# First front of a two-FFN, one-mixer layer: three groups routed before the shared expert starts, statistics of all tokens early, VectorE takes half of the inverse roots

## Chip, core and metric

The kernel runs on one core of a Trainium2 chip. The metric is the device time of one execution in microseconds (us), lower is better. Engines are called by the names of the profile: PE is TensorE, DVE is VectorE, ACT is ScalarE, POOL is GpSimd, SP is SyncE.

## What is computed

4096 tokens of 128 channels (16 sequences of 256) pass three residual steps, each on a layer norm of the tokens: half an FFN, a causal decaying mixer with two circular transforms, and half of the same FFN again.

```python
def ffn(x):                        # x: (4096, 128), already layer-normed
    logits = x @ router.T          # 8 experts
    idx = argmax(logits)           # one expert for each token
    h = silu(x @ gate[idx].T) * (x @ up[idx].T)          # 256 wide
    y = h @ down[idx].T
    ys = (silu(x @ w_gate_s.T) * (x @ w_up_s.T)) @ w_down_s.T   # shared expert, all tokens
    return y + ys

x = x + 0.5 * ffn(layernorm(x))
x = x + attn(layernorm(x))         # n + gate * corr(decay_scan(conv(n, bind)), unbind)
x = x + 0.5 * ffn(layernorm(x))
```

## The kernel before

Tokens are held in SBUF as 32 tiles of 128, and worked on in 8 groups of 4 tiles (`TPG = 4`, `G = 8`). Every engine has its program written out by hand, with semaphores between them. Each FFN has a **front** and an **expert part**. Here the front of the first FFN matters; it is the function `front(0, k)` of PE, ACT and DVE and `first_ffn(k)` of POOL, called for k from -3 (DVE), -1 (PE, ACT) and so on up to 7. For one group it does this:

- DVE `stats_of` or `moments` and `aggregate`: mean and variance of the four tiles (L591 to L602). In `choose` the four L591 of a later group stand between the linked steps of the routing, so that these hide each other's latency; `AHEAD = 3` says that group k+3 is measured while group k is routed.
- POOL `rstd`: `(variance + eps) ** -0.5` by one power instruction (L367) and the shift (L371).
- ACT `norm`: four normalised tiles `xn` (L463). PE `turn`: four transposes (L871). ACT `evac_rows`: the copy `xnT` (L478).
- PE: four products with the router (L905), semaphore `logits`. DVE `choose` (L662 to L668): the first best expert of each token as a one-hot matrix. PE: ranks of the tokens within their expert (L924 to L932). DVE `place_rows` (L677, L681): the row to which each token goes.
- POOL `scatter`: four indirect DMAs (L378) that put the group's rows into `dispatched`, sorted by expert.

The rank of the next group builds on the counts of this one, and the routing of group k+1 may start only after `place_rows` of group k, which frees the bank `rt`.

The **shared expert** is cut into 24 parts: for every group two halves of gate and up (`part` 0 and 1: PE L885 with two 512-column products, ACT silu L487, DVE product L639) and one down product (`part` 2: PE L893, DVE L607). They stand in the order `SHARED_PARTS`; `parts_at(k, i)` gives those before (`i = 0`) and behind (`i = 1`) the routing of group k. Before, groups 1 to 7 each take one part in either place, 14 in all (`EARLY`); the next five (up to `LATE = 19`) stand behind the front, and the others behind the expert part. The five and DVE's table chain (`block_experts`, `tables`, L750 to L778), which needs the counts of all tokens, are the last thing ahead of the expert part. There PE first waits for these five parts, since the banks are used again (first product L959); SP loads blocks of sorted rows when all scatters have landed.

ACT waits for POOL in `norm`, and every engine takes its instructions in the order written. SP issues the loads of x in four pieces (`X_LOADS`: group 0, group 1, groups 2 and 3, groups 4 to 7), between them the weights.

## Time and profile before

| | |
|---|---|
| median of 3 runs | 345.94 us (343.34 to 346.11) |
| the profiled execution's own time | 345.24 us |
| its span, first to last instruction | 343.5 us |
| mean granted TensorE clock | 0.931 |
| busy: PE, DVE, ACT, POOL | 273.2, 189.6, 160.2, 191.2 us |
| first scatter starts, last one of the first front ends | 13.67, 67.47 us |
| first product of the first expert part starts | 75.05 us |

The busy times are sums over the whole span. The change touches the first 75 us, so the times of the single instructions there tell more than the sums. A name after `<-` in square brackets is what ended an engine's idle time, as far as the profile can tell; `remote` stands where it found no instruction that did.

### The profile page before, as it was taken

The numbers are of one execution on the slowest core, as the hardware profiler recorded it, in microseconds if no ns is written. First come the engines' busy times: TensorE is split into PE (matmuls) and PEld (weight loads), VectorE is DVE, ScalarE is ACT, GpSimd is POOL, SyncE is SP. The second block draws the span as 40 slices with busy tenths as digits, with TensorE's granted clock in tenths as the row PEclk, the third lists the DMA queues.
The fourth block names the chain that finished last, engine by engine and source line by source line (L and its number), as shares of the span: only waits on it lengthen the run. The fifth ranks groups of instructions, "written<-read, shape, count | busy, mean of one in ns | idle before, by whom it ended". The sixth has DMA issues, their size and how long they took to land.

```text
span 343.5 us, 7913 instructions
## 1 busy us (share of the span) xinstructions
PE 273.2 (80%) x1804; PEld 217.7 (63%) x1804; DVE 189.6 (55%) x725; ACT 160.2 (47%) x375; POOL 191.2 (56%) x302
## 2 busy tenths in 40 slices
PE   7788991889799788895499889959797877969860
PEld 2465770559798678763386667735697766859540
DVE  5666640944444354436999898728353524534353
ACT  3534540146555455513599488501564635535210
POOL 6466775404576655662447888764057465655700
PEclk9899998599989999998859989998999999989996
DMA  7931111222222222119000100113222222222178
GB/s 194 379 146 43 40 50 47 88 56 64 63 65 74 65 62 78 56 47 240 5 3 25 41 32 32 49 47 96 58 63 73 65 60 62 70 62 64 41 226 268
DMA packets 34990, 28.34 MB, mean 83 GB/s; under 512 B 4784, under 2 KB 31792, under 8 KB 34704
## 3 DMA queue, kind: packets, MB, share of 16 engines
q1 hardware_dynamic: 25328, 16.06, 16.8%
q0 software_dynamic: 4544, 9.45, 7.6%
q10 hardware_dynamic: 5088, 2.50, 2.4%
q8 instruction: 11, 0.18, 0.2%
q14 instruction: 19, 0.16, 0.2%
HBM read 15.37 MB, written 12.62 MB: 81 GB/s over the span
## 4 chain that ended last, share of the span: by engine, by line
PE 25%; issue 19%; SPq 15%; POOL 11%; DVE 10%; another core or an unknown queue 7%; DMA 7%; ACT 3%; DVEq 1%; POOLq 0%; ACTq 0%
PE bank L959 9%; SPq L304 6%; POOL dispatched L378 6%; PE bank L885 5%; SPq L316 5%; PE bank L893 3%; DMA back<-returned 3%; PE bank L969 2%; PE bank L905 2%; DMA xs<-dispatched 2%; POOL returned L412 2%; POOL scale_f L367 2%; DVE st_f L591 2%; SPq L336 1%
## 5 line engine op out<-in xcount | busy, mean ns | idle before, releaser
L412 POOL DMA_INDIRECT returned<-ey,token x78 | 77.7, 996 | 66.5 <-DVE ey L807 34.0
L959 PE MATMUL bank<-xsT,wgu 128*128 128x128 f32 x624 | 87.3, 285 | 14.9 <-ACT xsT L531 6.0
L959 PEld LDWEIGHTS bank<-xsT,wgu 128*128 128x128 f32 x624 | 77.7, 196 | 19.6 <-issue 9.0
L378 POOL DMA_INDIRECT dispatched<-xn,slot x64 | 64.0, 1000 | 28.2 <-issue 17.7
L885 PE MATMUL bank<-xnT,gu 128*128 128x512 f32 x128 | 67.6, 659 | 2.9 <-issue 1.6
L801 DVE TENSOR_TENSOR eh<-eg,bank 128x256 f32<-128x256 f32 x78 | 32.8, 420 | 57.0 <-ACT eg L538 39.0
L538 ACT ACTIVATE eg<-bank 128x256 f32<-128x256 f32 x78 | 29.8, 382 | 58.1 <-PE bank L959 43.3
L969 PE MATMUL bank<-wdn,eh 128*128 128x128 f32 x312 | 48.7, 281 | 0.8 <-issue 0.7
L487 ACT ACTIVATE sg<-bank 128x512 f32<-128x512 f32 x32 | 18.9, 589 | 64.1 <-PE bank L885 29.2
L512 ACT ACTIVATE wgu<-gu 128x512 f32 x78 | 48.3, 624 | 0.6 <-issue 0.6
L969 PEld LDWEIGHTS bank<-wdn,eh 128*128 128x128 f32 x312 | 41.9, 196 | 1.8 <-issue 1.6
L893 PEld LDWEIGHTS bank<-dn,hs 128*128 128x128 f32 x256 | 33.0, 207 | 11.9 <-DVE hs L639 9.1
L893 PE MATMUL bank<-dn,hs 128*128 128x128 f32 x256 | 34.4, 291 | 6.2 <-DVE hs L639 5.7
L885 PEld LDWEIGHTS bank<-xnT,gu 128*128 128x128 f32 x128 | 23.9, 205 | 23.0 <-issue 22.0
L463 ACT ACTIVATE xn<-xres,shift_f,scale_f 128x128 f32<-128x128 f32 x64 | 26.3, 482 | 18.8 <-POOL shift_f L371 18.8
L785 DVE COPY wdn<-dn 128x256 f32 x78 | 23.5, 302 | 20.6 <-PE bank L969 19.3
L639 DVE TENSOR_TENSOR hs<-sg,bank 128x512 f32<-128x512 f32 x32 | 21.8, 682 | 11.7 <-ACT sg L487 11.6
L807 DVE COPY ey<-bank 128x128 f32<-128x128 f32 x78 | 22.2, 284 | 8.9 <-issue 4.9
L948 PE MATMUL bank<-ident,xs 128*128 128x128 f32 x80 | 18.1, 286 | 10.2 <-DMA xs<-dispatched 9.4
L405 POOL TENSOR_TENSOR token<-xs,to_replica 128x1 int32<-128x1 int32 x78 | 16.3, 209 | 13.0 <-issue 6.1
L905 PEld LDWEIGHTS bank<-routerT,xnT 128*128 128x128 f32 x128 | 17.0, 201 | 9.1 <-issue 7.4
L531 ACT ACTIVATE xsT<-bank 128x256 f32<-128x256 f32 x40 | 14.9, 372 | 12.6 <-PE bank L948 5.8
(102 smaller groups left out, 294.0 us busy)
## 6 DMA issues: line engine op xcount, KB each, us to landing
xs<-dispatched SPq DMA_DIRECT2D x80, 66.0 KB
back<-returned SPq DMA_DIRECT2D x16, 256.0 KB, 5.5
gu<-in_gu SPq DMA_DIRECT2D x1, 2048.0 KB
out<-xres ACTq DMA_DIRECT2D x8, 256.0 KB, 3.9
returned<-ey,token POOLq DMA_INDIRECT x78
dn<-in_dn SPq DMA_DIRECT2D x1, 1024.0 KB
dispatched<-xn,slot POOLq DMA_INDIRECT x64
dispatched<-pads SPq DMA_DIRECT2D x10, 66.0 KB
```

The source lines that it names most:

```text
L378: nc.gpsimd.indirect_dma_start(dispatched[:, :], bass.IndirectOffsetOnAxis(slot[:, i:i + 1], 0), xn[:, i, :], None, bounds_check=last_row) ...
L412: nc.gpsimd.indirect_dma_start(returned[:, :], bass.IndirectOffsetOnAxis(token[:, s:s + 1], 0), ey[:, s, :], None, bounds_check=last_back) ...
L463: nc.scalar.activation(dst[:, at * TPG + t, 0:C], xres[:, i, :], ACT.Identity, bias=shift[kind][:, i:i + 1], scale=scale[kind][:, i:i + 1] ...
L512: nc.scalar.activation(wgu[:, r, :], tile(gu, e), ACT.Copy).then_inc(blk_wgu, 1)
L538: nc.scalar.activation(eg[:, r, :], bank[4 + r][:, 0:H], ACT.Silu).then_inc(blk_silu, 1)
L785: nc.vector.tensor_copy(wdn[:, r, :], tile(dn[:].rearrange("p e h c -> p e (h c)"), e)).then_inc(blk_wdn, 1)
L801: nc.vector.tensor_tensor(eh[:, r, :], eg[:, r, :], bank[4 + r][:, H:2 * H], ALU.mult).then_inc(blk_mul, 1)
L885: last = nc.tensor.matmul(ps[:], gu[:, SHARED, at:at + P], xnT[:, g, :], start=True, stop=True)
L893: last = nc.tensor.matmul(o_ps[:, t * C:(t + 1) * C], hs[:, n % 2, h, t * P:(t + 1) * P], dn[:, SHARED, h, :], start=(h == 0), stop=(h == ...
L905: last = nc.tensor.matmul(rt[:, t * E:(t + 1) * E], xnT[:, k, t * P:(t + 1) * P], routerT[:], start=True, stop=True)
L959: last = nc.tensor.matmul(bank[4 + s % WR][:, i * P:(i + 1) * P], wgu[:, s % WR, i * P:(i + 1) * P], xsT[:, s // 2 % 2, s % 2, :], start=T ...
L969: last = nc.tensor.matmul(bank[2 + s % 2][:, 0:C], eh[:, s % WR, h * P:(h + 1) * P], wdn[:, s % WR, h * C:(h + 1) * C], start=(h == 0), st ...
```

## The change

It touches the first front alone, apart from counts of semaphores:

- `FILL` replaces one part on either side of each routing: in the first front groups 0, 1 and 2 take no shared part, groups 3, 4 and 5 two each, groups 6 and 7 three each (two before the routing, one behind). 12 parts stand in the front and seven behind it. In the second front the parts stay where they were.
- `STATS_AT`: the statistics of groups 0, 1, 2 are taken ahead of the loop as before, group 3 in the routing of group 0, groups 4 and 5 with group 1, groups 6 and 7 with group 2; the second one of each pair stands behind `place_rows`, all four instructions of L604 in a row.
- The inverse roots of groups 0 to 3 are POOL's, all before its first scatter. Those of groups 4 to 7 are computed by DVE in one chain of 12 linked steps over 16 columns (`rstd_of_rest`): a bit trick for the first guess, three Newton steps, the shift. ACT's `norm` of groups 4 to 7 waits for the whole chain. POOL has no root between its scatters any more.
- `prepare_attention` of DVE (with ACT's tanh and the product of the two keys on PE), and PE's wait for the shared weights, move from group 0 to group 3.
- SP issues all x loads, and then the weights of the shared expert.

```diff
-PER_STEP = 2
-EARLY = PER_STEP * (G - 1)
-LATE = EARLY + 5
+FILL = ((0, 0, 0, 2, 2, 2, 3, 3), (0, 2, 2, 2, 2, 2, 2, 2))
+EARLY = tuple(sum(fill) for fill in FILL)
+LATE = max(EARLY) + 5
+STATS_AT = {-3: (0,), -2: (1,), -1: (2,), 0: (3,), 1: (4, 5), 2: (6, 7)}
+SHARED_FROM = 3
+NEWTON = 3
+MAGIC = float(0x5F3759DF)
+BY_DVE = 4
+DVE_RSTD_STEPS = 3 + 3 * NEWTON
...
-            return SHARED_PARTS[PER_STEP * (k - 1) + i:][:1] if 1 <= k < G else []
+            if not valid(k):
+                return []
+            first, middle = sum(FILL[f][:k]), (FILL[f][k] + 1) // 2
+            return SHARED_PARTS[first + i * middle:first + (FILL[f][k] if i else middle)]
...
             load_x(0)
             load_x(1)
             sp.dma_start(routerT[:], router_in).then_inc(routes_in, 16)
+            load_x(2)
+            load_x(3)
             sp.dma_start(gu[:, SHARED, :], gu_in[:, SHARED, :]).then_inc(shared_in, 16)
             sp.dma_start(dn[:, SHARED, :, :], dn_in[:, SHARED, :, :]).then_inc(shared_in, 16)
-            load_x(2)
...
-            load_x(3)
...
             def first_ffn(k):
                 if k < 0:
-                    rstd("f", k + AHEAD, k + AHEAD)
-                elif k in (1, 3):
-                    rstd("f", k + 2, k + 2, groups=2)
-                elif k == 4:
-                    rstd("f", k + 3, k + 3)
-                if valid(k):
+                    rstd("f", k + BY_DVE, k + BY_DVE)
+                else:
                     scatter(0, k)
...
+                if kind == "f" and BY_DVE <= n < G:
+                    act.wait_ge(dve_rstd, DVE_RSTD_STEPS)
...
+            def rstd_of_rest():
+                at = slice(BY_DVE * TPG, NT)
+                v, y, step = var["f"][:, at], scale["f"][:, at], [0]
+                def link(ins):
+                    step[0] += 1
+                    ins.then_inc(dve_rstd, 1)
+                    if step[0] < DVE_RSTD_STEPS:
+                        dve.wait_ge(dve_rstd, step[0])
+                dve.wait_ge(stats["f"], G)
+                link(nc.vector.tensor_scalar(square[:].bitcast(I32), v.bitcast(I32), 1, None,
+                                             ALU.logical_shift_right))
+                link(nc.vector.tensor_scalar(y.bitcast(I32), square[:].bitcast(I32), -1.0, MAGIC, ALU.mult, ALU.add))
+                for _ in range(NEWTON):
+                    link(nc.vector.tensor_tensor(square[:], y, y, ALU.mult))
+                    link(nc.vector.scalar_tensor_tensor(out=square[:], in0=square[:], scalar=-0.5, in1=v,
+                                                        op0=ALU.mult, op1=ALU.mult))
+                    link(nc.vector.scalar_tensor_tensor(out=y, in0=square[:], scalar=1.5, in1=y,
+                                                        op0=ALU.add, op1=ALU.mult))
+                link(nc.vector.tensor_tensor(shift["f"][:, at], y, minus_mean["f"][:, at], ALU.mult))
...
-                kind, later = ("f", k + AHEAD) if f == 0 else ("a", k + 4)
+                kind, laters = ("f", STATS_AT.get(k, ())) if f == 0 else ("a", (k + 4,))
+                later = laters[0] if laters else G
...
                 if valid(k):
                     place_rows(n, k, q)
+                for more in laters[1:]:
+                    stats_of(kind, more, more)
+                if f == 0 and k == max(STATS_AT):
+                    rstd_of_rest()
...
             def first_ffn(k):
                 front(0, k)
-                if k == 0:
+                if k == SHARED_FROM:
                     prepare_attention()
...
             pe.wait_ge(routes_in, 16)
+            for k in range(0, SHARED_FROM):
+                front(0, k)
             pe.wait_ge(shared_in, 16 * 2)
-            front(0, 0)
+            front(0, SHARED_FROM)
```

On POOL, this is what follows the constants before (L378 is a scatter, x4 a group):

```order
L367 TENSOR_TENSOR scale_f<-var_f,minus_half 128x4
L371 TENSOR_TENSOR shift_f<-scale_f,minus_mean_f 128x4
L378 DMA dispatched<-xn,slot 33792x132 x4
L367 TENSOR_TENSOR scale_f<-var_f,minus_half 128x8
L371 TENSOR_TENSOR shift_f<-scale_f,minus_mean_f 128x8
L378 DMA dispatched<-xn,slot 33792x132 x8
L367 TENSOR_TENSOR scale_f<-var_f,minus_half 128x8
L371 TENSOR_TENSOR shift_f<-scale_f,minus_mean_f 128x8
L378 DMA dispatched<-xn,slot 33792x132 x4
L367 TENSOR_TENSOR scale_f<-var_f,minus_half 128x4
L371 TENSOR_TENSOR shift_f<-scale_f,minus_mean_f 128x4
L378 DMA dispatched<-xn,slot 33792x132 x16
```


And now (L392 is the scatter):

```order
L381 TENSOR_TENSOR scale_f<-var_f,minus_half 128x4
L385 TENSOR_TENSOR shift_f<-scale_f,minus_mean_f 128x4
L381 TENSOR_TENSOR scale_f<-var_f,minus_half 128x4
L385 TENSOR_TENSOR shift_f<-scale_f,minus_mean_f 128x4
L392 DMA dispatched<-xn,slot 33792x132 x32
```


The power instructions between the scatters are gone; a fourth pair stands ahead of the first scatter.

On DVE, this stands behind the routing step of group 2 before (place and slot of group 2, the shared part, the first step of group 3):

```order
L677 TENSOR_TENSOR place<-bank2,chosen 128x32
L681 TENSOR_REDUCE slot<-place 128x4
L607 SCALAR_TENSOR_TENSOR xres<-bank3,xres 128x512
L662 TENSOR_REDUCE top<-bank2 128x4
L591 BN_STATS st_f<-xres 128x6
L663 TENSOR_TENSOR cand<-bank2,top 128x32
```


And now, in the same place (the end of `stats_of(7)` and `rstd_of_rest` lie between slot of group 2 and `top` of group 3):

```order
L611 BN_AGGR mv_f<-st_f 128x2 x4
L614 TENSOR_SCALAR var_f<-mv_f 128x4
L615 TENSOR_SCALAR minus_mean_f<-mv_f 128x4
L630 TENSOR_SCALAR square<-var_f 128x16
L632 TENSOR_SCALAR scale_f<-square 128x16
L634 TENSOR_TENSOR square<-scale_f 128x16
L635 SCALAR_TENSOR_TENSOR square<-square,var_f 128x16
L637 SCALAR_TENSOR_TENSOR scale_f<-square,scale_f 128x16
L634 TENSOR_TENSOR square<-scale_f 128x16
L635 SCALAR_TENSOR_TENSOR square<-square,var_f 128x16
L637 SCALAR_TENSOR_TENSOR scale_f<-square,scale_f 128x16
L634 TENSOR_TENSOR square<-scale_f 128x16
```


Four more rows of that chain follow, and then `top` of group 3 with nothing between its steps. The routing of group 3 stands behind statistics and Newton steps in DVE's order.

On PE, from the ranks of the last group to the expert part (L948), before:

```order
L932 MATMUL bank2<-region,ones 128x32
L885 MATMUL bank4<-xnT,gu 128x512
L885 MATMUL bank5<-xnT,gu 128x512
L893 MATMUL bank3<-dn,hs 128x128 x8
L885 MATMUL bank6<-xnT,gu 128x512
L885 MATMUL bank7<-xnT,gu 128x512
L885 MATMUL bank4<-xnT,gu 128x512
L885 MATMUL bank5<-xnT,gu 128x512
L893 MATMUL bank3<-dn,hs 128x128 x8
L948 MATMUL bank0<-ident,xs 128x128 x2
```


And now:

```order
L973 MATMUL bank2<-region,ones 128x32
L934 MATMUL bank3<-dn,hs 128x128 x8
L926 MATMUL bank6<-xnT,gu 128x512
L926 MATMUL bank7<-xnT,gu 128x512
L926 MATMUL bank4<-xnT,gu 128x512
L926 MATMUL bank5<-xnT,gu 128x512
L934 MATMUL bank3<-dn,hs 128x128 x8
L926 MATMUL bank6<-xnT,gu 128x512
L926 MATMUL bank7<-xnT,gu 128x512
L926 MATMUL bank4<-xnT,gu 128x512
L926 MATMUL bank5<-xnT,gu 128x512
L934 MATMUL bank3<-dn,hs 128x128 x8
L989 MATMUL bank0<-ident,xs 128x128 x2
```


Behind the last ranks one more gate and up half and one more down product stand ahead of the expert part.

## Rows read from the trace of the kernel before

**Rows 1.** The chain that ended last, in order of time: start, length, what.

```profile
48.94 10.95 another core or an unknown queue
...
75.05 2.07 PE bank L959 x16
```

**Rows 2.** Timeline of GpSimd (POOL): start, length, instruction, [idle before, releaser].

```profile
13.67 1.20 POOL L378 DMA_INDIRECT dispatched<-xn,slot  x1 [2.06 <-DVE slot L681]
...
41.41 1.05 POOL L367 TENSOR_TENSOR scale_f<-var_f,minus_half 128x4 f32<-128x4 f32 x1
...
57.01 0.97 POOL L378 DMA_INDIRECT dispatched<-xn,slot  x1 [0.30 <-issue]
62.45 0.97 POOL L378 DMA_INDIRECT dispatched<-xn,slot  x1 [4.47 <-DVE slot L681]
```

**Rows 3.** Timeline of TensorE (PE) in the first front.

```profile
9.74 1.03 PE L905 MATMUL bank<-routerT,xnT 128*128 128x8 f32 x8 [0.78 <-ACT xnT L478]
...
39.85 0.95 PE L905 MATMUL bank<-routerT,xnT 128*128 128x8 f32 x8
40.66 2.03 PE L893 MATMUL bank<-dn,hs 128*128 128x128 f32 x16
42.52 0.60 PE L871 MATMUL bank<-ident,xn 128*128 128x128 f32 x4
...
43.12 1.96 PE L885 MATMUL bank<-xnT,gu 128*128 128x512 f32 x4
44.92 0.95 PE L905 MATMUL bank<-routerT,xnT 128*128 128x8 f32 x8
...
50.80 1.96 PE L885 MATMUL bank<-xnT,gu 128*128 128x512 f32 x4
...
61.52 3.76 PE L885 MATMUL bank<-xnT,gu 128*128 128x512 f32 x4
```

**Rows 4.** Timeline of VectorE (DVE), first groups.

```profile
5.53 0.87 DVE L591 BATCH_NORM_STATS2 st_f<-xres 128x6 f32<-128x128 f32 x4
...
6.93 0.16 DVE L602 TENSOR_SCALAR minus_mean_f<-mv_f 128x4 f32<-128x4 f32 x1
...
10.87 0.19 DVE L662 TENSOR_REDUCE top<-bank 128x4 f32<-128x32 f32 x1 [0.62 <-PE bank L905]
...
12.95 0.18 DVE L677 TENSOR_TENSOR place<-bank,chosen 128x32 f32<-128x32 f32 x1
```

**Rows 5.** Timeline of VectorE, last group, tables and first weights.

```profile
59.91 0.19 DVE L662 TENSOR_REDUCE top<-bank 128x4 f32<-128x32 f32 x1 [10.33 <-remote]
...
62.77 0.16 DVE L750 TENSOR_SCALAR n_up<-bank 128x8 int32<-128x8 f32 x1
...
68.01 0.68 DVE L639 TENSOR_TENSOR hs<-sg,bank 128x512 f32<-128x512 f32 x1
...
72.29 0.69 DVE L639 TENSOR_TENSOR hs<-sg,bank 128x512 f32<-128x512 f32 x1 [1.03 <-ACT sg L487]
...
74.32 0.68 DVE L607 SCALAR_TENSOR_TENSOR xres<-bank,xres 128x512 f32<-128x512 f32 x1
```

**Rows 6.** Timeline of ScalarE (ACT).

```profile
36.03 1.65 ACT L463 ACTIVATE xn<-xres,shift_f,scale_f 128x128 f32<-128x128 f32 x4 [3.25 <-POOL shift_f L371]
...
59.97 0.60 ACT L487 ACTIVATE sg<-bank 128x512 f32<-128x512 f32 x1 [11.15 <-remote]
```

**Rows 7.** Timeline, second FFN front, last group.

```profile
225.53 1.96 PE L885 MATMUL bank<-xnT,gu 128*128 128x512 f32 x4
...
229.01 0.97 POOL L378 DMA_INDIRECT dispatched<-xn,slot  x1 [0.30 <-issue]
230.00 0.19 DVE L662 TENSOR_REDUCE top<-bank 128x4 f32<-128x32 f32 x1 [5.95 <-remote]
```

**Rows 8.** Windows: length, busy time (instructions) by engine, granted clock, DMA share, GB/s.

```profile
9.30:12.70 3.40, 1.90 (x18) 1.52 (x19) 2.68 (x22) 3.07 (x9) 1.20 (x2) 1.00 1.11 349
12.70:16.10 3.40, 3.40 (x12) 1.75 (x10) 2.29 (x11) 0.98 (x3) 2.13 (x2) 0.53 1.00 424
```

More of the change, by code:

```diff
@@ L446, in _ @@
             pool.wait_ge(const_made, 3)
-            for k in range(-AHEAD, 1):
-                first_ffn(k)
-            for k in range(1, G):
+            for k in range(-BY_DVE, G):
                 first_ffn(k)
@@ L496, in front @@
                     norm("f", n + 1, k + 1, xn, k + 1)
-                for g, part in parts_at(k, 0):
+                for g, part in parts_at(f, k, 0):
                     shared(f, g, part)
@@ L501, in front @@
                     norm("a", k + 3, k + 3, xa, (k + 3) % 2)
-                for g, part in parts_at(k, 1):
+                for g, part in parts_at(f, k, 1):
                     shared(f, g, part)
@@ L514, in before_experts @@
             def before_experts(f):
-                for g, part in SHARED_PARTS[EARLY:LATE - 1]:
+                for g, part in SHARED_PARTS[EARLY[f]:LATE - 1]:
                     shared(f, g, part)
@@ L693, in front @@
                     stats_of(kind, later, later)
-                for g, part in parts_at(k, 0):
+                for g, part in parts_at(f, k, 0):
                     shared(f, g, part)
@@ L708, in before_experts @@
                 tables()
-                for g, part in SHARED_PARTS[EARLY:LATE - 1]:
+                for g, part in SHARED_PARTS[EARLY[f]:LATE - 1]:
                     shared(f, g, part)
@@ L898, in front @@
                 n, q = f * G + k, k % 2
-                for g, part in parts_at(k, 0):
+                for g, part in parts_at(f, k, 0):
                     shared(f, g, part)
@@ L913, in front @@
                     last.then_inc(mixed, 1)
-                for g, part in parts_at(k, 1):
+                for g, part in parts_at(f, k, 1):
                     shared(f, g, part)
@@ L1000, in _ @@
             pe.wait_ge(routes_in, 16)
+            for k in range(0, SHARED_FROM):
+                front(0, k)
             pe.wait_ge(shared_in, 16 * 2)
-            front(0, 0)
+            front(0, SHARED_FROM)
             pe.wait_ge(small_in, 16 * 4)
             nc.tensor.matmul(tp["a"][:, 0:C], hank_u[:], hank_b[:], start=True, stop=True).then_inc(mix_raw, 1)
-            for k in range(1, G):
+            for k in range(SHARED_FROM + 1, G):
                 front(0, k)
-            for g, part in SHARED_PARTS[EARLY:LATE]:
+            for g, part in SHARED_PARTS[EARLY[0]:LATE]:
                 shared(0, g, part)
@@ L1015, in _ @@
             steps(lambda k: front(1, k), 3)
-            for g, part in SHARED_PARTS[EARLY:LATE]:
+            for g, part in SHARED_PARTS[EARLY[1]:LATE]:
                 shared(1, g, part)
```

30 lines of the change are left out of this document (19 added, 11 removed).

## The prediction

> **What bounds the first front now.** I read the chain of waits for the first 80 us first, then the timeline of each engine beside it. The expert part starts at 75.05 [rows 1]; all that the change touches lies ahead of that, so its worth is how far this moment moves. The largest piece of the chain is 10.95 us that it gives to nobody [rows 1]. What happens there is in the timelines: PE has issued the router products of group 7 by 50.80, when the next products start, and these end at 52.76 [rows 3]. VectorE, which only needs the router products, starts `top` at 59.91, ScalarE, which needs the other ones, its silu at 59.97 [rows 5, 6]. For group 0 `top` starts 1.13 after the first router product starts [rows 3, 4], 0.1 behind the last one's end, so it could have begun at about 51.0 here: it is 8.9 us late, and ScalarE 7.2. No instruction's end stands at 59.9. I can't name the cause; I call it late signals from TensorE. In the second front the same group shows it again: PE goes on at 225.53, `top` starts at 230.00, 4.3 late [rows 7].
>
> Without the lateness POOL would be the bound. Its scatters run from 13.67 to 67.47, 53.8 us; one takes 0.97 and 0.30 to the next [rows 2], so 32 take 40.8, and 13.0 are roots and waits. POOL finishes group 6 at 57.98 and then waits 4.47 for the slots of group 7 [rows 2], which are late only because of the signals. Both ends thus matter: the scatters' end, and the chain PE and VectorE have behind the last routing.
>
> **POOL's part.** A fourth root ahead of the first scatter costs what a root and a shift take, 1.05 for the power [rows 2] and some 0.25. The statistics of group 3 end just ahead of place of group 0 at 12.95 [rows 4], so the first scatter starts at 14.4 to 14.6 instead of 13.67: +0.9. From there nothing but scatters is left: 28 of them end at 14.6 + 35.8 = 50.4, if slots are there in time. POOL's gain is real but worth nothing unless the rest follows.
>
> **Early groups.** In a round without shared parts the products of group 0 start at 9.74 and place starts at 12.95 and ends 0.18 later [rows 3, 4], so the next round starts at 13.15, a period of 3.4. Group 1: `top` at 14.3, place 16.4, slot done 16.7; behind it VectorE now has the statistics of group 5, 1.56 (5.53 to 7.09) [rows 4], to 18.3. Group 2's products are ready at 17.7, so it waits 0.6 for VectorE: `top` 18.3, place 2.08 later (10.87 to 12.95) at 20.4, slot 20.7, statistics of group 7 to 22.3.
>
> **The Newton chain.** No such chain is in the trace. Its nearest rows are the chain of tables, 16 linked steps in 5.24 (62.77 to 68.01), 0.33 each, some of them over 320 columns [rows 5]; the six steps of a routing, with the ranks on PE, take 1.61 (59.91 to 61.52) [rows 3, 5], about 0.22 a step. Twelve steps over 16 columns cost 2.6 to 3.9; I take 3.2, since the first two work on integers and the others are as narrow as a routing step. That is 25.5. It is wholly exposed: VectorE takes `top` of group 3 behind it, and ScalarE's `norm` of group 4 waits for it, 1.65 [rows 6], to 27.1. The transposes and ranks of group 3 are queued behind that norm on PE: 27.5. So group 3 is routed at about 28.0. POOL doesn't care, it is busy with groups 0 to 2 until 14.6 + 15.3 = 29.9. PE does: between 20 and 27 it has only two halves of the shared expert to do.
>
> **PE's rounds from group 4.** A round with one down product and one half takes 5.07 (39.85 to 44.92); in it the down product 1.86, and a half 1.80 (43.12 to 44.92) [rows 3]. One with a part more takes 6.87. The half ahead of group 4 runs 27.6 to 29.4, the products of group 4 start at 29.4, of group 5 at 34.5, of group 6 at 41.3, of group 7 at 48.2. `prepare_attention` moves behind group 3 on VectorE, about 1.9, and ends at 30.5, as the products of group 4 are ready: it costs nothing there, and up to 1 if the Newton chain takes 3.9. `top` of group 7 is at 49.3 and its slots are there by 51.4, 1.0 after POOL is free. The last scatter ends at about 56.4, against 67.47.
>
> **Behind the routing.** This is what the change pays with: seven parts, not five. On VectorE the table chain starts 2.86 behind `top` (59.91 to 62.77) [rows 5]; now with one product more, 3.45: 52.7 to 58.0. Meanwhile PE does the down product of group 3 and two halves, 5.5 from 50.9, and stands from 56.4, as the product of group 4 is queued behind the tables: add and product end at 59.3. Then PE has down 4 (61.2) and a half (63.0); its silu and product take 1.4 (64.4), hidden by the next half (64.8); down 5 ends at 66.7. The last product of VectorE starts at 65.6, and from there to the first expert product it is 2.76 (72.29 to 75.05) [rows 1, 5]: 68.4. The blocks of sorted rows are no bound: scatters end 11 us earlier. **Sum: 68.4 - 75.05 = -6.65**, with signals on time.
>
> **Loads.** x for groups 4 to 7 comes ahead of the shared weights. VectorE needs it at 14, PE the shared weights at 20. In the stretch 9.30 to 16.10 the queues move 349 to 424 GB/s [rows 8], so the 0.4 MB that come later are about 1 us of it: nothing either way.
>
> **The clock.** From 9.30 to 12.70 PE was busy 1.90 of 3.40, with just this pattern of router products, transposes and ranks, and behind that the granted clock fell to 0.53 of 2.4 GHz, the lower level of 1.2 [rows 8]. It came back after a stretch of products without a gap. Now three rounds look like that, so I expect the low level until the shared parts start at about 20.6; a half of the shared expert then takes 3.76 instead of 1.96 [rows 3]. Both halves of group 3 lie beside the Newton chain, with room (20.6 to 27.1), so it costs nothing while the clock is back by 27. The Trainium skill ("TensorE: Matmul & The Clock Gate", section "HAM oscillation — how this bites in real kernels") describes a kernel whose short bursts between waits drop back to half rate each time and pay again in every round. By that rule the waits for `norm` of group 4 would keep PE low, and the sum would lose what the rival below has.
>
> **How late will the signals be?** Both late cases ended about when POOL's unbroken run of scatters ended: POOL done 57.98 and 229.98, `top` 59.91 and 230.00 [rows 2, 5, 7], 1.9 and 0.0 later. Two cases prove no link. If there is one, POOL is done with group 6 at 50.4 now, so `top` of group 7, due 49.3, would come by 50.4 to 52.3: 1.1 to 3.0 late; I take 2.5, which also stands for small delays in earlier rounds, no longer absorbed by POOL's backlog. Everything behind moves with it: -6.65 + 2.5 = **-4.1**. The profiled execution took 345.24, the median is 345.94; its front is taken to be typical, and the gain goes off the median: **341.8**.
>
> **Rivals.**
> *On time:* no lateness at group 7, since PE's order there is another (a half between down product and router products). 345.94 - 6.65 = 339.3. For it: most groups show none. Against: both fronts had it at group 7.
> *As in the second front:* 4.3 late, 345.94 - 6.65 + 4.3 = 343.6.
> *Slower:* the lateness belongs to group 7 whatever POOL does, and is 8.9 again. Two parts more lie behind it, so the place of the loss is between `top` of group 7 and the first expert product: 15.1 before (59.91 to 75.05), 19.1 now (49.3 to 68.4). PE idles long enough for the clock to fall; the three parts that the tables hide take 10.2, not 5.5, against 8.4 of cover: +1.8. 68.4 + 8.9 + 1.8 = 79.1, so +4.1: 350.0. It decides from a lateness of about 5 to 6.6 on.
> *Clock low past 27:* two or three products at the low level at 1.8 more each, 3.0 to 5.4, of which the round times keep nearly all; or the Newton chain at 3.9 with its shift of later rounds. With 2.5 of lateness 345 to 346: no gain.
> *Scatters alone bound:* the expert part moves as the scatters' end, 11.1: 334.8. Against it speak the seven parts, 12.8 of PE work at 1.80 and 1.86 each, which can't end before 63.7.
>
> **Chances.** Forecast (340.3 to 343.0) 0.33; on time 0.25; 4.3 late 0.15; clock or long chain 0.10; slower 0.10; scatters alone 0.04; the rest is spread. The three runs of before lie 2.8 apart, so 1% (3.5) is about what can be told from no change. Below 342.5 lie the forecast's larger part, on time and scatters: 0.56; above 349.4 0.09. The range leaves out the slower case and the scatters: 338.0 to 347.0.
>
> **What would show it.** Right: first scatter at 14.5, no root between scatters; a wait of ScalarE for the last Newton step until 25 or 26; PE's router products of group 7 at 48; table chain from 52.7 to 55; first expert product at 68 to 71. Wrong: `top` of group 7 more than 5 us behind its products; a granted clock of 0.5 past 27; PE waiting for VectorE in groups 4 to 6; or the gain at the start of the expert part given back by its end, for which I see no reason, since from there on nothing is changed but counts.

## The result, and the profile after

The changed kernel takes 353.17 us (median of four runs, 351.9 to 360.16), the kernel before beside it 346.02 (four runs, 343.34 to 348.49). The ratio is **1.021, interval 1.015 to 1.027: slower**, by 1.5 to 2.7%, where 341.8 was forecast. Some executions are disturbed and take some per cent longer, here the one of 360.16: they count in the medians, but in no ratio. The profiled execution took 351.9, its span is 350.1 (343.5 before), its granted clock 0.915 (0.931). The first expert product starts at 82.51 instead of 75.05, 7.5 later, and from there to the first product of the second expert part it is 169.7 us after and 169.6 before. The whole loss thus lies in the first front.

The timeline of POOL, the changed kernel:

```profile
14.63 1.20 POOL L392 DMA_INDIRECT dispatched<-xn,slot  x1 [0.18 <-issue]
...
28.89 0.97 POOL L392 DMA_INDIRECT dispatched<-xn,slot  x1 [0.31 <-issue]
34.33 0.97 POOL L392 DMA_INDIRECT dispatched<-xn,slot  x1 [4.47 <-DVE slot L717]
...
41.95 0.97 POOL L392 DMA_INDIRECT dispatched<-xn,slot  x1 [2.81 <-DVE slot L717]
...
50.88 0.97 POOL L392 DMA_INDIRECT dispatched<-xn,slot  x1 [0.30 <-issue]
56.56 0.97 POOL L392 DMA_INDIRECT dispatched<-xn,slot  x1 [4.71 <-DVE slot L717]
...
66.69 0.97 POOL L392 DMA_INDIRECT dispatched<-xn,slot  x1 [5.33 <-DVE slot L717]
```

Twelve scatters stand in a row from 14.63 to 29.86, then four, eight (41.95 to 51.85), four and four, with a wait for slots ahead of each piece. Before, once the first scatter was out, POOL waited for slots twice, 1.49 ahead of group 2 and 4.47 ahead of group 7 [rows 2]; now four times, 17.3 us.

PE, which the slots come from, and VectorE:

```profile
24.79 0.95 PE L946 MATMUL bank<-routerT,xnT 128*128 128x8 f32 x8
...
33.95 3.68 PE L926 MATMUL bank<-xnT,gu 128*128 128x512 f32 x4
...
49.66 0.95 PE L946 MATMUL bank<-routerT,xnT 128*128 128x8 f32 x8
...
56.02 3.78 PE L934 MATMUL bank<-dn,hs 128*128 128x128 f32 x16 [0.87 <-DVE hs L675]
...
62.56 0.95 PE L946 MATMUL bank<-routerT,xnT 128*128 128x8 f32 x8
...
82.51 0.71 PE L1000 MATMUL bank<-xsT,wgu 128*128 128x128 f32 x4 [1.43 <-DVE xres L643]
```

```profile
19.61 0.19 DVE L698 TENSOR_REDUCE top<-bank 128x4 f32<-128x32 f32 x1 [0.40 <-PE bank L946]
...
22.48 0.19 DVE L713 TENSOR_TENSOR place<-bank,chosen 128x32 f32<-128x32 f32 x1 [0.70 <-PE bank L973]
...
24.60 0.17 DVE L614 TENSOR_SCALAR var_f<-mv_f 128x4 f32<-128x4 f32 x1 [0.51 <-DVE mv_f L611]
...
24.88 0.17 DVE L630 TENSOR_SCALAR square<-var_f 128x16 int32<-128x16 int32 x1
...
26.03 0.17 DVE L634 TENSOR_TENSOR square<-scale_f 128x16 f32<-128x16 f32 x1 [0.76 <-DVE scale_f L632]
...
29.82 0.17 DVE L639 TENSOR_TENSOR shift_f<-scale_f,minus_mean_f 128x16 f32<-128x16 f32 x1
31.79 0.19 DVE L698 TENSOR_REDUCE top<-bank 128x4 f32<-128x32 f32 x1 [1.80 <-remote]
...
53.42 0.19 DVE L698 TENSOR_REDUCE top<-bank 128x4 f32<-128x32 f32 x1 [6.16 <-remote]
...
63.55 0.19 DVE L698 TENSOR_REDUCE top<-bank 128x4 f32<-128x32 f32 x1 [6.67 <-PE bank L946]
...
67.02 0.16 DVE L791 TENSOR_SCALAR n_up<-bank 128x8 int32<-128x8 f32 x1
```

Read them as pairs. The router products of group 3 end at 25.74, its `top` starts at 31.79: the signal is 6.0 late, and for the last 1.8 of that VectorE, free from 29.99, waits for nothing else. Group 6: 50.61 and 53.42, 2.8 late. Group 7, 9.0 late before (router products end at 50.94, `top` at 59.91), is on time: 63.51 and 63.55. The lateness has not gone. It has moved ahead and come apart into two pieces, 8.8 together against 9.0. It is also between VectorE's own linked steps: those of the Newton chain stand 0.21 apart where all is well, and here with up to 0.76 of idle time, so that the chain takes 5.1 (24.88 to 29.99).

The windows show what each pause of PE costs besides (length, busy time by engine, granted clock, DMA share, GB/s):

```profile
12.70:23.00 10.30, 7.87 (x44) 6.19 (x44) 7.00 (x53) 3.89 (x10) 7.75 (x9) 0.50 0.74 300
23.00:33.40 10.40, 6.31 (x26) 2.99 (x24) 4.87 (x29) 3.08 (x9) 5.34 (x6) 0.83 0.12 41
33.40:39.00 5.60, 5.60 (x23) 3.52 (x20) 2.75 (x10) 2.24 (x6) 3.76 (x4) 0.57 0.11 36
39.00:56.00 17.00, 14.18 (x93) 9.89 (x91) 7.75 (x29) 6.79 (x15) 7.90 (x9) 0.98 0.11 36
56.00:62.50 6.50, 6.48 (x20) 4.78 (x21) 0.84 (x3) 0.00 (x0) 3.88 (x4) 0.53 0.14 45
62.50:83.00 20.50, 16.47 (x90) 10.80 (x89) 13.38 (x39) 5.52 (x10) 4.49 (x6) 1.00 0.23 63
```

At 33.4 and at 56 the clock is at the lower level, 1.2 GHz, again, each time behind a stretch in which PE stood and waited (3.39 idle up to 30.96 for `norm` of group 4, which waits for the stretched Newton chain; 1.97 and 0.87 before 56.02 for VectorE, whose `top` of group 6 was late). A half of the shared expert then takes 3.68 (33.95), not 1.96, and a down product 3.78 (56.02), not 2.03.

### The profile page after: what moved, and what is told of

Its sections match the earlier page's. It is cut to its first block, busy times and chain, and to the rows that moved or that the text cites. A ratio compares the mean times of both kernels' runs of the same rounds, so it can differ in the third digit from the quotient of the medians.

```text
span 350.1 us, 7926 instructions
## 1 busy us (share of the span) xinstructions
PE 281.2 (80%) x1804; PEld 220.0 (63%) x1804; DVE 192.1 (55%) x737; ACT 160.6 (46%) x375; POOL 186.8 (53%) x298
## 4 chain that ended last, share of the span: by engine, by line
PE 36%; DVE 14%; issue 14%; SPq 12%; POOL 7%; another core or an unknown queue 6%; DMA 5%; ACT 3%; DVEq 1%; ACTq 0%; POOLq 0%
PE bank L1000 14%; PE bank L926 6%; PE bank L1010 5%; SPq L315 5%; SPq L327 3%; POOL dispatched L392 3%; PE bank L946 3%; PE bank L934 3%; DMA back<-returned 2%; PE bank L989 2%; DVE st_f L604 2%; DVE xres L643 2%; PE bank L912 1%; DMA xs<-dispatched 1%
## 5 line engine op out<-in xcount | busy, mean ns | idle before, releaser
L1000 PE MATMUL bank<-xsT,wgu 128*128 128x128 f32 x624 | 85.9, 282 | 19.5 <-ACT xsT L544 11.7
L1000 PEld LDWEIGHTS bank<-xsT,wgu 128*128 128x128 f32 x624 | 76.7, 194 | 24.2 <-issue 14.4
L392 POOL DMA_INDIRECT dispatched<-xn,slot x64 | 63.8, 998 | 37.5 <-DVE slot L717 20.5
L926 PE MATMUL bank<-xnT,gu 128*128 128x512 f32 x128 | 70.9, 688 | 2.1 <-issue 1.9
L926 PEld LDWEIGHTS bank<-xnT,gu 128*128 128x128 f32 x128 | 25.6, 220 | 24.6 <-issue 24.6
L934 PEld LDWEIGHTS bank<-dn,hs 128*128 128x128 f32 x256 | 31.9, 201 | 12.6 <-DVE hs L675 10.9
L826 DVE COPY wdn<-dn 128x256 f32 x78 | 23.8, 305 | 18.4 <-PE bank L1010 15.1
L946 PEld LDWEIGHTS bank<-routerT,xnT 128*128 128x128 f32 x128 | 19.4, 223 | 9.4 <-issue 7.7
L989 PE MATMUL bank<-ident,xs 128*128 128x128 f32 x80 | 19.2, 290 | 5.7 <-DMA xs<-dispatched 4.1
```

What stands on the lines that cost most here:

```text
L392: nc.gpsimd.indirect_dma_start(dispatched[:, :], bass.IndirectOffsetOnAxis(slot[:, i:i + 1], 0), xn[:, i, :], None, bounds_check=last_row) ...
L926: last = nc.tensor.matmul(ps[:], gu[:, SHARED, at:at + P], xnT[:, g, :], start=True, stop=True)
L934: last = nc.tensor.matmul(o_ps[:, t * C:(t + 1) * C], hs[:, n % 2, h, t * P:(t + 1) * P], dn[:, SHARED, h, :], start=(h == 0), stop=(h == ...
L946: last = nc.tensor.matmul(rt[:, t * E:(t + 1) * E], xnT[:, k, t * P:(t + 1) * P], routerT[:], start=True, stop=True)
L989: last = nc.tensor.transpose(bank[pair % 2][:, s % 2 * P:(s % 2 + 1) * P], xs[:, s, 0:C], ident[:])
L1000: last = nc.tensor.matmul(bank[4 + s % WR][:, i * P:(i + 1) * P], wgu[:, s % WR, i * P:(i + 1) * P], xsT[:, s // 2 % 2, s % 2, :], start=T ...
```

## The experiments

**The theory (A):** scatters issued without a break, one per 1.28 us, hold back the signals of TensorE, and some of VectorE's, once several are out, until 0 to 2 us behind the last. (Router signals due within the first four scatters of a run were on time, those due at the seventh were late.) Before, the roots between the scatters and one wait for slots were such breaks:

```profile
20.27 1.67 POOL L367 TENSOR_TENSOR scale_f<-var_f,minus_half 128x8 f32<-128x8 f32 x1 [1.56 <-DVE minus_mean_f L602]
...
29.15 0.97 POOL L378 DMA_INDIRECT dispatched<-xn,slot  x1 [1.49 <-DVE slot L681]
...
33.97 1.68 POOL L367 TENSOR_TENSOR scale_f<-var_f,minus_half 128x8 f32<-128x8 f32 x1
```

With the root at 41.41 [rows 2] the runs were 4, 4, 4, 4, 12 and 4 scatters long, and only the 12 had a router signal more than 0.7 late in it. The change takes all roots from between them. **Rivals:** the lateness belongs to PE's own order of work; to POOL's work of any kind; to a pile of transfers under way; or the loss comes from the moved shared parts or the moved loads.

"Breaks" are powers on POOL that go into a tile which nobody reads. The kernel before was run again beside them, the first eight experiments on one chip and the last four on another, with medians of 348.08 (first four experiments), 346.94 (next four) and 352.31 (last four), so kernels are compared by their ratio to it. "Late" is from the end of a group's router products to its `top`, where VectorE stood idle ahead of it, `E` the start of the first expert product.

| kernel | us | ratio (interval) | late, first front | last scatter ends | E |
|---|---|---|---|---|---|
| before | 346.02 | | 9.0 (group 7) | 67.5 | 75.05 |
| changed | 353.17 | 1.021 (1.015 to 1.027) | 6.0 (3), 2.8 (6) | 71.7 | 82.51 |
| e1 scatters last | 375.28 | 1.072 (1.057 to 1.087) | none | 96.6 | 101.78 |
| e2 breaks | 344.54 | 0.995 (0.989 to 1.001) | none | 62.5 | 71.18 |
| e3 old parts | 354.25 | 1.024 (1.013 to 1.036) | 4.9 (7) | 73.2 | 79.92 |
| e4 loads | 350.79 | 1.010 (1.005 to 1.015) | 8.6 (7) | 70.5 | 77.76 |
| e5 before, breaks | 345.9 | 0.994 (0.990 to 0.998) | none | 67.0 | 72.24 |
| e6 short breaks | 351.09 | 1.014 (1.009 to 1.020) | 4.5 (3), 2.8 (6) | 66.1 | 76.62 |
| e7 powers in a run | 375.98 | none, one run | none | 96.5 | 102.59 |
| e8 two in flight | 353.03 | none, runs too far apart | 1.6 (5), 6.4 (6) | 72.3 | 83.81 |
| e9 roots on POOL | 348.49 | 0.982 (0.976 to 0.988) | 1.1 (5) | 63.6 | 74.02 |
| e10 both fronts | 343.58 | **0.979 (0.973 to 0.984)** | none | 63.6 | 69.40 |
| e11 narrow breaks | 346.7 | 0.989 (0.983 to 0.995) | none | 63.9 | 69.51 |
| e12 parts moved back | 346.28 | 0.987 (0.981 to 0.993) | none | 63.5 | 69.64 |

**e1: no scatter while routing.**

```diff
             for k in range(-BY_DVE, G):
+                if k == 0:
+                    pool.wait_ge(slotted, G)
                 first_ffn(k)
```

> The changed kernel, with GpSimd waiting for the slots of all eight groups before its first scatter; the same scatters in the same order. Theory A (an unbroken run of scatters of more than about six holds back the signals of TensorE, and some of VectorE, until 1.4 to 2 us after the run's end): no late signal while the groups are routed, so the Newton chain takes 12 steps at 0.21, about 2.8 us in place of 5.1, `top` of group 3 starts at about 28, `top` of group 7 at 49 to 51 in place of 63.6; behind it 32 scatters take 41 us, so the last ends near 93 and the whole is 20 us slower than the changed kernel, with late signals in that run at the earliest 6 us into it. Theory B (TensorE's own dense stream of short products makes its signals late, whatever GpSimd does): the routing products of groups 3 and 6 are again followed by `top` 3 to 6 us late, and `top` of group 7 stays above 58.

VectorE, then POOL:

```profile
26.75 0.19 DVE L700 TENSOR_REDUCE top<-bank 128x4 f32<-128x32 f32 x1 [0.69 <-PE bank L948]
...
52.64 0.19 DVE L700 TENSOR_REDUCE top<-bank 128x4 f32<-128x32 f32 x1 [3.74 <-PE bank L948]
...
67.28 0.69 DVE L645 SCALAR_TENSOR_TENSOR xres<-bank,xres 128x512 f32<-128x512 f32 x1 [4.58 <-remote]
```

```profile
55.81 1.20 POOL L392 DMA_INDIRECT dispatched<-xn,slot  x1 [41.39 <-DVE slot L719]
```

With the same orders on PE, VectorE and ScalarE all eight groups are on time (0.1 at most), the Newton chain takes 2.5, and `top` of group 7 stands at 52.64 instead of 63.55. So PE's order is not the cause. And once the 32 scatters run, from 55.8, the signals are late again: a down product that ends at 64.21 is seen at 67.28. The time itself, 375, is that of scatters behind the routing.

**e2: a break ahead of every group's scatters.**

```diff
                 else:
+                    if k:
+                        nc.gpsimd.tensor_tensor(cols(rest, k), cols(var["f"], 0), minus_half[:], ALU.pow)
                     scatter(0, k)
```

> The changed kernel with one more instruction on GpSimd ahead of the scatters of groups 1 to 7 of the first front: a power of four columns (1.05 us) into a tile that nobody reads, so that no run of scatters is longer than four. Theory A: the late signals at groups 3 and 6 are gone or under 1 us, `top` of group 7 at 50 to 54, the first expert product at 70 to 74 in place of 82.5, the whole 8 to 12 us faster than the changed kernel and 1 to 4 faster than the one before, although GpSimd has 7 us more to do. Theory B: late signals stay, time within 2 us of the changed kernel. Theory C (only the end of a long backlog matters, not the breaks): the lateness moves to other groups, time between the two.

POOL, then VectorE, then PE's first expert product:

```profile
19.51 1.04 POOL L402 TENSOR_TENSOR rest<-var_f,minus_half 128x4 f32<-128x4 f32 x1
20.75 1.05 POOL L393 DMA_INDIRECT dispatched<-xn,slot  x1 [0.20 <-issue]
```

```profile
26.60 0.19 DVE L701 TENSOR_REDUCE top<-bank 128x4 f32<-128x32 f32 x1 [0.49 <-PE bank L949]
...
45.51 0.19 DVE L701 TENSOR_REDUCE top<-bank 128x4 f32<-128x32 f32 x1 [3.38 <-PE bank L949]
...
52.70 0.19 DVE L701 TENSOR_REDUCE top<-bank 128x4 f32<-128x32 f32 x1 [3.74 <-PE bank L949]
```

```profile
71.18 0.49 PE L1003 MATMUL bank<-xsT,wgu 128*128 128x128 f32 x2 [1.43 <-DVE xres L646]
```

Seven useless powers of 1.05 us on the engine that issues the scatters make the front 11.3 us shorter than the changed kernel's. No router signal is late, and the last scatter ends 9.2 earlier although there is more to do. The whole loss against before, and 3.9 us more, hangs on these breaks. The time is 344.54, no different from before by its interval, where 1 to 4 us less were expected.

**e3: the shared parts as before** (`FILL[0]` and `SHARED_FROM`).

```diff
-SHARED_FROM = 3
+SHARED_FROM = 0
-FILL = ((0, 0, 0, 2, 2, 2, 3, 3), (0, 2, 2, 2, 2, 2, 2, 2))
+FILL = ((0, 2, 2, 2, 2, 2, 2, 2), (0, 2, 2, 2, 2, 2, 2, 2))
```

> The changed kernel with the places of the shared expert's parts and of the mixer's preparation as before (FILL of the first front as that of the second, SHARED_FROM 0): statistics early, Newton chain on VectorE and the x loads stay changed. If the moved parts are the cause (seven parts behind the routing, TensorE idle in the first groups), it is back at the kernel before or faster, 340 to 346. If late signals from unbroken scatters are the cause, most of the loss stays, 348 to 354, since GpSimd has no root between its scatters here either.

It is as slow as the changed kernel, but of other things. `top` of group 0 is at 14.4, 3.5 later, since PE's wait for the shared weights now stands ahead of it. Slots come slower than POOL could send them at first, so the scatters run in pieces of four with waits between them, and the Newton chain beside them takes 2.5. The lateness is back at group 7, whose signal is due at the fifth scatter of a run of eight. The position of the lateness goes with the scatters' run and not with the group.

**e4: the kernel before with only the loads moved.**

```diff
+            load_x(2)
+            load_x(3)
             sp.dma_start(gu[:, SHARED, :], gu_in[:, SHARED, :]).then_inc(shared_in, 16)
```

> The kernel before with the x loads of the changed one (all x pieces ahead of the shared expert's weights) and nothing else. All theories: within 1 us of the kernel before; statistics of group 2 start at 7.2 in place of 8.7, and the shared weights come up to 2 us later than the 13.1 at which TensorE first uses them, which would cost at most 2 us.

PE:

```profile
12.00 1.85 PE L905 MATMUL bank<-routerT,xnT 128*128 128x8 f32 x8 [3.10 <-DMA dn<-in_dn]
```

PE of this kernel waits for the shared weights ahead of group 0, so the moved loads cost 2.3 at once (9.74 before, [rows 3]), with the products at the lower clock 3.1 at `top`, 2.7 at `E`. I had expected less. In the changed kernel nobody waits for them until group 3, and group 0 is on time.

**e5: the kernel before with breaks ahead of groups 5, 6 and 7.**

```diff
                     rstd("f", k + 3, k + 3)
+                elif k > 4:
+                    nc.gpsimd.tensor_tensor(cols(rest, k), cols(var["f"], 0), minus_half[:, 0:TPG], ALU.pow)
```

> The kernel before with one power of four columns (1.05 us) on GpSimd ahead of the scatters of groups 5, 6 and 7 of the first front, and nothing else, so that its run of twelve scatters (42.9 to 58.0) becomes three of four. Theory A (a run of scatters without a break holds the signals of TensorE): the lateness of 9.0 us at group 7 goes, `top` of group 7 at 51 to 52, and the last scatter, three powers later but no longer waiting for slots, ends at 66 to 67; the first expert product, bound by the scatters, at 71 to 72 in place of 75.05: 3 to 4 us faster than before. Theory B (the lateness is a matter of TensorE's stream or of group 7's place): no gain, 0 to 3 us slower by the powers.

POOL and VectorE:

```profile
48.53 1.05 POOL L391 TENSOR_TENSOR rest<-var_f,minus_half 128x4 f32<-128x4 f32 x1
49.77 1.05 POOL L379 DMA_INDIRECT dispatched<-xn,slot  x1 [0.19 <-DVE slot L684]
```

```profile
51.70 0.19 DVE L665 TENSOR_REDUCE top<-bank 128x4 f32<-128x32 f32 x1 [1.34 <-PE bank L908]
```

The unexplained 10.95 of the chain [rows 1] is gone: `top` of group 7 starts 8.2 earlier. Only 2.8 of that reach the first expert product, because now the scatters are the bound (the last ends at 67.0). Three instructions make the kernel before 0.6% faster (0.2 to 1.0), 2 us, where 3 to 4 were expected.

**e6: short breaks**, a product of 0.22 us in place of each power of e2 (`ALU.mult`, not `ALU.pow`).

> As the kernel with breaks, but the instruction between two groups' scatters is a product of four columns, 0.2 us, in place of the power of 1.05: the gap between two scatters there is 0.6 to 0.9 in place of 0.3 us. If any other instruction of GpSimd that is done ends the hold, the lateness is gone as well, `top` of group 7 at 52 to 53, first expert product near 69 to 70 and the time 1 to 2 us below the kernel with breaks. If what counts is the idle time in which something drains, the lateness is back in part, `top` of group 7 at 54 to 62, time between that kernel's and the changed one's.

```profile
19.55 0.22 POOL L402 TENSOR_TENSOR rest<-var_f,minus_half 128x4 f32<-128x4 f32 x1
```

```profile
30.15 0.19 DVE L701 TENSOR_REDUCE top<-bank 128x4 f32<-128x32 f32 x1 [2.48 <-remote]
```

POOL keeps one scatter per 1.31 us in the mean, and the signals are late by 4.5 and 2.8 again. That there is an instruction between scatters does not help; the time that it takes does.

**e7: e1 with 36 powers in a run on POOL while the groups are routed.**

```diff
                 if k == 0:
+                    pool.wait_ge(slotted, 1)
+                    for i in range(36):
+                        nc.gpsimd.tensor_tensor(cols(rest, i), cols(var["f"], 0), minus_half[:], ALU.pow)
                     pool.wait_ge(slotted, G)
```

> The kernel that scatters last, with 36 powers of four columns (some 40 us) on GpSimd, without a break, while the groups are routed. If it is the scatters (their descriptors or their transfers) that hold the signals, there is no late signal until the first scatter, `top` of group 3 at 26.7 and of group 7 at 52.6 as without the powers, and the time is that of the kernel that scatters last or a few us more, as the powers end near 53. If it is any unbroken run of work on GpSimd, `top` of groups 3 to 7 comes 3 to 9 us late.

Nothing is late: `top` of groups 3 and 7 at 26.6 and 52.5, as in e1. So POOL's computing without scatters does not hold the signals. It is the scatters that do.

**e8: at most two scatters in flight.** Each of the first front waits until the one two before it has landed, by three semaphores in turn.

```diff
+                    if f == 0 and i > 1:
+                        pool.wait_ge(land[(i - 2) % 3], 16 * ((i - 2) // 3 + 1))
                     nc.gpsimd.indirect_dma_start(
```

> The changed kernel, where each scatter of the first front waits until the transfer of the one two before it has landed, by three semaphores in turn. A scatter lands some 1.15 us after its instruction ends and the next one takes 1.27, so this wait costs nearly nothing (at most 0.1 us each) and the run stays without a break. If transfers that are piled up behind one another hold the signals, the lateness goes and the time is 342 to 346. If it is the making of descriptors on GpSimd itself, or the wait costs nothing because there never was a pile, the time stays at the changed kernel's, 351 to 355.

PE and VectorE:

```profile
46.49 0.95 PE L953 MATMUL bank<-routerT,xnT 128*128 128x8 f32 x8
```

```profile
53.83 0.19 DVE L705 TENSOR_REDUCE top<-bank 128x4 f32<-128x32 f32 x1 [7.58 <-remote]
```

While the weights load, the waits stretch the scatters, and groups 0 to 4 are on time. From 30.75 to 51.63 they start at 1.39 us in the mean, since a wait adds up to 0.5 to the usual 0.30, more than the 0.1 expected, and the signals are 1.6 and then 6.4 late. A pile of more than two transfers is not needed for it. The times say less: three of the four runs took 352.56 to 355.2, the fourth 344.38, which is what was expected if the lateness went. That one left no trace, so it is open whether its signals were on time.

**e9: the change without the Newton chain.** POOL makes the roots of groups 4 to 7 ahead of the scatters of 1 to 4, where they serve as breaks, and powers that nobody reads ahead of 5 to 7.

```diff
+                    if k and valid(k + 3):
+                        rstd("f", k + 3, k + 3)
+                    elif k:
+                        nc.gpsimd.tensor_tensor(cols(rest, k), cols(var["f"], 0), minus_half[:], ALU.pow)
                     scatter(0, k)
...
-                if f == 0 and k == max(STATS_AT):
-                    rstd_of_rest()
```

> The changed kernel without its Newton chain: GpSimd takes the roots of groups 4 to 7 too, one each ahead of the scatters of groups 1 to 4, and a power that nobody reads ahead of those of groups 5, 6 and 7. So every break of the kernel with breaks is there, four of them as real work. Theory A: no late signal in the first front; 2.6 us of chain go from in front of group 3 on VectorE, but TensorE is on the low clock there, so `top` of group 3 moves from 26.6 to 24 to 25, of group 7 from 52.7 to 49 to 51, the first expert product from 71.2 to 68 to 69.5, with the scatters (end 62.5 and 5.3 more) as the next bound at 67.8. Time 1.5 to 3 us below the kernel with breaks, 3 to 6 below before. If the Newton chain costs nothing once signals are on time, it is within 1 us of the kernel with breaks.

It beats the kernel before by 1.8%, but its trace misses what was expected: the signal of group 5 is 1.1 late (38.60 and 39.68) though the scatters start only every 1.60 us there, `top` of group 7 stands at 53.47, not 49 to 51, and `E` at 74.02, not 68 to 69.5. PE is at the lower clock for most of 26 to 30 and again from 63.45, where a down product takes 3.27. That the Newton chain is worth 1.5 to 3 us is thus not shown. Its second front still has group 7 late, 5.5; all other kernels up to here, before and after among them, have it 4.2 to 4.7 late there.

**e10: e9 with breaks ahead of groups 6 and 7 of the second front too.**

```diff
+                if k >= 6:
+                    nc.gpsimd.tensor_tensor(cols(rest, G + k), cols(var["f"], 0), minus_half[:], ALU.pow)
                 if valid(k):
                     scatter(1, k)
```

> As the one with GpSimd's roots, with two powers more in the second front, ahead of the scatters of groups 6 and 7, where two groups' scatters ran without a break and the router products of group 7 were signalled 4.3 us late in the kernel before. Theory A: that lateness goes, second front 3 to 4 us shorter from the first to the second expert part, less 0 to 1.3 that the powers cost; time 2 to 3.5 us below the one without them. If the second front's lateness has another cause, no gain.

POOL, VectorE and PE:

```profile
222.22 1.04 POOL L410 TENSOR_TENSOR rest<-var_f,minus_half 128x4 f32<-128x4 f32 x1
```

```profile
223.36 0.19 DVE L697 TENSOR_REDUCE top<-bank 128x4 f32<-128x32 f32 x1 [1.47 <-PE bank L943]
```

```profile
69.40 0.79 PE L997 MATMUL bank<-xsT,wgu 128*128 128x128 f32 x5 [0.68 <-ACT xsT L543]
```

No router signal is late in either front. This has the lowest ratio, 2.1% below before (2.7 to 1.6%) and 4.2% below the changed kernel by the two ratios, but its interval overlaps those of e9, e11 and e12. The gain of the second front is not shown either. From `E` to the first product of the second expert part it takes 170.1 us, 2.5 less than e9 (3 to 4 were expected), but the kernel before takes 169.6 with a signal that is 4.3 late in it.

**e11: a power of one column (0.58 us) behind every second scatter** of the first front, on the changed kernel.

```diff
+                    if f == 0 and i % 2:
+                        nc.gpsimd.tensor_tensor(rest[:, i:i + 1], var["f"][:, 0:1], minus_half[:, 0:1], ALU.pow)
```

> The changed kernel with a power of one column (some 0.55 us) behind every second scatter of the first front: two scatters in about 3.0, the same mean pace of 1.5 us a scatter as with a break of 1.24 at every fourth, but no gap above 0.8. If what counts is the mean pace (something behind the scatters is worked off at a rate between one in 1.54 us, which was on time, and one in 1.31 to 1.41, which was late), no late signal, and time as the kernel with breaks, 342 to 346. If it takes one gap of a microsecond or more for it to drain, signals are late at groups 3, 6 or 7 by 2 us and more, and the time is 348 or above.

```profile
38.60 0.58 POOL L397 TENSOR_TENSOR rest<-var_f,minus_half 128x1 f32<-128x1 f32 x1
39.37 1.05 POOL L393 DMA_INDIRECT dispatched<-xn,slot  x1 [0.18 <-issue]
```

Two scatters now take 3.1, 1.55 each, as in e2 (four in 6.15), with gaps half as long, and the router signals are on time (`top` of group 3 follows VectorE's own chain without a pause). With e6 and e8 beside it, the mean pace counts: late at 1.28, 1.31 and 1.39, on time at 1.54 and 1.55. The 1.1 at group 5 of e9, at 1.60, does not fit this and stays unexplained; e10 has the same first front and no late signal in it.

**e12: e10 with one shared part each in groups 1 and 2** and PE's wait for the shared weights ahead of group 1.

```diff
-FILL = ((0, 0, 0, 2, 2, 2, 3, 3), (0, 2, 2, 2, 2, 2, 2, 2))
+FILL = ((0, 1, 1, 2, 2, 2, 3, 3), (0, 2, 2, 2, 2, 2, 2, 2))
```

> As the one with powers in both fronts, but groups 1 and 2 take one half of the shared expert each (14 parts in the front, five behind it, as in the kernel before). TensorE has 3.6 us less behind the routing and no longer idles ahead of group 3, and its clock comes back sooner. First expert product at 67.8 to 69 (bound by the scatters) if the other was at 68 to 69.5: 0 to 2 us faster than that. Against it: a half ahead of group 1's routing takes 3.8 at the low clock, which moves slots of group 1 and 2 later, to about 21 and 26, just as GpSimd wants them; if that exceeds 1 us, the gain is lost.

`top` of groups 1 and 2 comes 2 and 4 us later than in e10 and `E` is the same within 0.3: no gain. Putting two parts back into the groups that had none gives nothing.

## Why the prediction was wrong

**What bounds the front** was read rightly, the 9 us of late signals and POOL behind them; e5 shows both at once.

**POOL's part:** first scatter 14.63 (14.4 to 14.6 forecast), 12 scatters to 29.86 (29.9). Right, and this unbroken run is what I counted as a gain.

**Early groups:** `top` of group 1 at 15.26 and of 2 at 19.61, forecast 14.3 and 18.3. The period is 4.35, not 3.4, mostly because at the lower clock the eight router products take 1.85, not 1.03. I forecast that clock and priced the shared parts by it, but left the rounds at full speed: 1.3 too little.

**The Newton chain:** 3.2 forecast, 2.5 without late signals (e1, e2, e3), 5.1 here. It ended at 29.99, not 25.5: 1.3 from the rounds, 1.3 from VectorE's waits ahead of the chain, 0.70 ahead of `place` of group 2 for PE's signal and 0.51 in the statistics of group 7 (the chain starts at 24.88 against 23.53 in e2), 2.6 within it, less 0.7 over-estimated.

**PE's rounds and the sum:** `top` of group 7 stands at 63.55, not 49.3. e2, the same orders with signals on time, has 52.70. So of the 14.25 missing, 3.4 were missing with signals on time too, mostly by the lower clock, and 10.85 the late signals. These build up as 5.2 to group 3 (31.79 against 26.60), 2.7 more at group 6 (53.42 against 45.51, 7.9 in all), and 2.9 between groups 6 and 7, mostly by the clock that fell behind it.

**Behind the routing:** 19.0 from `top` to the first expert product, 19.1 forecast; the tables start 3.47 behind `top`, 3.45 forecast. Right. Against before, where it is 15.1, the front has paid 3.8 there, and the other 3.6 of the 7.5 lost are the later `top`.

**Loads:** nothing in the changed kernel, as forecast, though 3 us where they meet the old wait (e4).

**The clock:** low until the shared parts start, as forecast, but back by 27 only in some executions. With signals on time the windows of e2 and of e10 read:

```profile
20.00:26.00 6.00, 5.18 (x19) 2.83 (x17) 5.39 (x37) 0.60 (x1) 4.87 (x6) 0.50 0.18 63
26.00:32.00 6.00, 6.00 (x22) 3.31 (x23) 3.13 (x13) 3.92 (x10) 4.87 (x6) 0.66 0.15 48
```

```profile
20.00:26.00 6.00, 5.19 (x22) 2.79 (x21) 3.73 (x29) 2.80 (x6) 4.82 (x6) 0.66 0.20 66
26.00:32.00 6.00, 6.00 (x40) 4.26 (x40) 4.72 (x19) 3.21 (x8) 4.84 (x6) 1.00 0.13 45
```

e9 has e10's first front and the clock of e2, so the kernel does not decide it alone; `top` of group 7 is at 49.8 in e10 and 53.5 in e9. The same holds for e2 and e11, which give PE the same work in the same order: in e11 the clock is back before 26 and `E` is at 69.51, 1.1 behind the forecast's 68.4 with signals on time; in e2 it is at 71.18. The rival "clock low past 27" was thus there too, worth about 1.7 between these two. In the changed kernel the clock was back by 24.8 and fell again at 33.4 (0.57) and at 56 (0.53), each time behind waits of PE. The rule of the Trainium skill that the prediction weighed, "TensorE: Matmul & The Clock Gate", section "HAM oscillation — how this bites in real kernels", agrees with these two falls. It does not tell e2 from e10, where PE is equally busy from 20 to 26 (5.18 and 5.19 us).

**The step that failed** is "How late will the signals be?". It took 2.5 at group 7 and none at group 3, by the thought that lateness ends with the run of scatters. That part holds: `top` comes 1.9 and 1.6 behind the ends of the two long runs (29.86 and 51.85). What I missed is the other end of the same observation. A run makes the lateness, and the change, by taking the roots off POOL, turns 4 + 4 + 4 scatters at the start, beside which no router signal was more than 0.7 late before, into 12. What the runs showed in its place is 6.0 at group 3, 2.8 at group 6 and none at group 7, together with the clock 10.85 us of `top` of group 7, where 2.5 stood in the sum. I looked for lateness where it had been, at group 7, and not at which groups would now fall into a long run; that most groups showed none, as the rival "on time" says, was a reason to ask what else was different beside group 7. The rival that ended slower put the lateness at group 7 too: its sign came true, its place did not. Of the named signs of being wrong, a clock of 0.5 past 27 and PE waiting for VectorE in groups 4 to 6 came; a late `top` of group 7 did not.

**What the change is worth without this** can be read from e2 against e5, both with breaks: `E` at 71.18 and 72.24, and ratios 0.995 and 0.994. It is about 1 us at `E` in one trace of each, less than the clock alone makes between e2 and e11, and nothing that the times tell apart. The forecast of -6.65 against before was nearly all the lateness going away, which e5 gets alone, up to the scatters' bound.

**Open:** what holds the signals back. The scatters' pace decides; POOL's computing and a pile of more than two transfers are not needed. Whether it is the writing of their descriptors, the transfers' own signals or the records of the profile was not told apart, and no run scatters less data at the same pace. Every execution here was recorded by the profiler while it was timed, so the last can't be excluded. From the first expert product to that of the second part it was 168.9 to 174.6 us in these kernels, 172.3 in e2 and 169.7 in the changed one. This spread, which ate 2.5 of e2's gain of 11.3 over it, was not followed.

## What to carry to other kernels

When a trace shows a wait that nothing ends (`remote`, or "another core or an unknown queue"), ask what the other engines do in that stretch that they don't do elsewhere, and try to move that before building on it. One useless instruction there is a cheap trial. Work that looks like overhead between an engine's DMA issues may be what keeps the other engines' signals on time, so a change that frees it needs a new look at every group that falls beside the longer run. And where a forecast names a lower clock, it must go into every product of that stretch, the short ones too.

## What the runs showed of the hardware that was not expected

- GpSimd's indirect scatters (128 rows each), issued one per 1.28 to 1.39 us for longer than four or five scatters, go with TensorE semaphore signals that are 1.6 to 9.0 us late and VectorE ones that are 0.3 to 0.8 late; at one per 1.54 to 1.60 all router signals of the first front but one (1.1, e9) were on time in five kernels (e2, e9 to e12).
- Linked VectorE steps over 128x16 stand 0.21 us apart, integer ones too: 12 in 2.5 (e1, e2, e3).
- The same front had TensorE's clock back before 26 in one kernel and after 26 in another (e10, e9); `top` of group 7 differs by 3.7 us, of which the late signal of group 5 is at most 1.1.
